# A GRU scan with a ternary FFN on one core: a bias tile loaded earlier, and ScalarE seeding the candidate's bank two steps sooner

## The reference, cut to what matters

```python
def cell(h, x):
    gi = x @ W_ih + b_ih
    gh = h @ W_hh + b_hh
    i_r, i_z, i_n = jnp.split(gi, 3, axis=-1)
    h_r, h_z, h_n = jnp.split(gh, 3, axis=-1)
    r = jax.nn.sigmoid(i_r + h_r)
    z = jax.nn.sigmoid(i_z + h_z)
    n = jnp.tanh(i_n + r * h_n)
    h_new = (1.0 - z) * n + z * h
...
wq_gu = ternary_quant(w_gate_up)      # groups of 64: mean |w| is the scale, q in {-1, 0, 1}
gate, up = jnp.split(x @ wq_gu.T, 2, axis=-1)
h = jax.nn.silu(gate) * up
out = rms_norm(h) @ ternary_quant(w_proj).T
x = x + out
```

## Time and profile before

| What | Value |
| --- | --- |
| median of 3 runs | 346.22 us (346.09 to 346.31) |
| the profiled execution | 346.3 us |
| its span, first to last instruction | 344.5 us |
| PE busy | 339.4 us (99%) |
| DVE busy | 233.6 us (68%) |
| ACT busy | 222.8 us (65%) |
| POOL busy | 184.0 us (53%) |
| granted TensorE clock, mean | 1.000 |

### The profile page before, as it was taken

One profiled execution on the slowest core, in us unless ns is written; L12 is line 12 of the kernel. 1 busy time (PEld: TensorE's weight loads), 2 busy tenths in 40 slices (PEclk: granted clock), 3 DMA queues, 4 the chain that ended last, 5 costly groups with the idle time before them and its releaser, 6 DMA issues.

```text
span 344.5 us, 5631 instructions
## 1 busy us (share of the span) xinstructions
PE 339.4 (99%) x2059; PEld 295.2 (86%) x2059; DVE 233.6 (68%) x462; ACT 222.8 (65%) x438; POOL 184.0 (53%) x156
## 2 busy tenths in 40 slices
PE   8999999999999999999999999999999999999996
PEld 4889988788988889888888889888888888888895
DVE  7578788899677565755667554875558555664866
ACT  5768888886756757555766656566564655756662
POOL 2315571465825446255454446444472554799694
PEclk9999999999999999999999999999999999999999
DMA  7994000045001000140001000010000100010101
GB/s 240 319 410 192 3 0 2 0 148 220 1 2 62 2 0 0 44 142 2 0 0 63 0 2 0 2 63 0 2 0 2 60 1 2 0 64 1 57 6 61
DMA packets 7891, 18.72 MB, mean 54 GB/s; under 512 B 564, under 2 KB 4788, under 8 KB 7352
## 3 DMA queue, kind: packets, MB, share of 16 engines
q1 hardware_dynamic: 7176, 17.97, 13.9%
q10 hardware_dynamic: 688, 0.39, 0.4%
HBM read 14.17 MB, written 4.19 MB: 53 GB/s over the span
## 4 chain that ended last, share of the span: by engine, by line
PE 94%; DVE 3%; ACT 1%; issue 1%; DVEq 0%
PE ps_ffn L1105 30%; PE ps_out L1143 16%; PE ps_rz L1017 7%; PE ps_rz L1022 7%; PE ps_rz L1018 7%; PE ps_n L1017 3%; PE ps_n L1022 3%; PE ps_n L1018 3%; PE ps_rz L1105 2%; PE ps_ffn L1270 2%; PE ps_t L1098 1%; PE ps_ffn L1017 1%; PE ps_ffn L1022 1%; PE ps_ffn L1018 1%; PE ps_n L1055 1%
## 5 line engine op out<-in xcount | busy, mean ns | idle before, releaser
L354 POOL TENSOR_TENSOR hid_lo<-work,hid_hi 128x512 fp32r<-128x512 f32 x62 | 81.7, 1317 | 103.6 <-ACT hid_hi L452 99.6
L1105 PE MATMUL ps_ffn<-st_hi,wguT 128*128 128x512 f32 x236 | 93.7, 397 | 0.3 <-DVE work L737 0.3
L1105 PE MATMUL ps_ffn<-st_lo,wguT 128*128 128x512 f32 x236 | 92.7, 393 | 0.0
L361 POOL TENSOR_TENSOR sq_sum<-sq_sum,work 128x512 f32<-128x512 f32 x55 | 73.2, 1331 | 1.8 <-ACT work L466 0.6
L737 DVE TENSOR_TENSOR work<-work,ps_ffn 128x512 f32<-128x512 f32 x55 | 37.6, 683 | 31.5 <-ACT work L448 31.5
L452 ACT CAST hid_hi<-work 128x512 fp32r<-128x512 f32 x63 | 38.8, 616 | 23.0 <-DVE work L747 23.0
L1105 PEld LDWEIGHTS ps_ffn<-st_hi,wguT 128*128 128x128 f32 x236 | 44.4, 188 | 8.3 <-DVE work L737 0.9
L1105 PEld LDWEIGHTS ps_ffn<-st_lo,wguT 128*128 128x128 f32 x236 | 44.5, 189 | 7.3
L747 DVE TENSOR_TENSOR work<-work,ps_ffn 128x512 f32<-128x512 f32 x63 | 43.2, 686 | 4.7 <-PE ps_ffn L1105 2.8
L1143 PEld LDWEIGHTS ps_out<-wpT,hid_hi 128*128 128x128 f32 x240 | 35.8, 189 | 3.7
L1143 PE MATMUL ps_out<-wpT,hid_lo 128*128 128x256 f32 x240 | 38.8, 284 | 0.0
(11 more groups left out here) (226 smaller groups left out, 716.0 us busy)
## 6 DMA issues: line engine op xcount, KB each, us to landing
out_dram<-o_st SPq DMA_DIRECT2D x7, 512.0 KB, 2.6
xT_all<-in_x_dram SPq DMA_DIRECT2D x1, 3072.0 KB, 17.6
x_ring<-in_x_dram SPq DMA_DIRECT2D x1, 3072.0 KB, 11.5
x_ring<-in_L_ffn_w_gate_up_dram SPq DMA_DIRECT2D x4, 512.0 KB, 8.9
x_ring<-in_L_ffn_w_proj_dram SPq DMA_DIRECT2D x2, 512.0 KB, 11.6
x_ring<-in_x_dram SPq DMA_DIRECT2D x1, 1024.0 KB, 5.4
work<-in_L_cond_W_ih_dram SPq DMA_DIRECT2D x3, 256.0 KB, 4.4
work<-in_L_cond_W_hh_dram SPq DMA_DIRECT2D x3, 256.0 KB, 4.6
```

What stands on the lines that cost most here:

```text
L354: nc.gpsimd.tensor_tensor(hid_lo[:, j % RING], hid[:, j % 2], f32(hid_hi[:, j % RING]), ALU.subtract).then_inc(hid_lo_ok, 1)
L361: nc.gpsimd.tensor_tensor(sq_sum[:], sq_sum[:], hid_sq[:, j % 2], ALU.add).then_inc(sq_added, 1)
L1105: mm = pe.matmul(bank, w, group_state(part, G, k), start=(k == 0 and i == 0), stop=(k == KD - 1 and i == 1))
```

## The change

Three things are done. The two DMAs of the n bias tile are issued before units 0 and 1 of the FFN weights and before the inputs of steps 4 to 7. ScalarE's `seed_n` starts at t = 0, that is for the bank of step 2, in place of step 4; TensorE's bias rows for n stay only for steps 0 and 1, and its input products for n wait for `n_seed` from step 2 on. The two halves of unit 0's signs, which stood where the two added seeds now stand, move: the first to behind `q_abs_of(0)` in step 0, the second to behind the r gate in step 2.

```diff
             load_inputs(2, 4, ld_x2)
+            for i, b in enumerate((b_ih, b_hh)):
+                sp.dma_start(bias[:, 1, i * D:(i + 1) * D], b[2 * D:G3].partition_broadcast(P)).then_inc(ld_bias_n, 16)
             load_unit(0)
             load_unit(1)
             load_inputs(4, LEAD, ld_x4)
-            for i, b in enumerate((b_ih, b_hh)):
-                sp.dma_start(bias[:, 1, i * D:(i + 1) * D], b[2 * D:G3].partition_broadcast(P)).then_inc(ld_bias_n, 16)
...
                 elif u >= 2:
                     q_weights(u - 2)
+                elif t:
+                    first_signs(1)
                 if t == 0:
                     n_gate(t)
                     z_gate(t)
                     q_abs_of(0)
+                    first_signs(0)
...
                 input_hi(t + 2)
-                if t < 2:
-                    first_signs(t)
-                elif t < LEAD - 1:
-                    if t == 2:
+                if t < LEAD - 1:
+                    if t == 0:
                         act.wait_ge(ld_bias_n, 32)
                     seed_n(t + 2)
...
             def input_n_part(t, part):
 
-                if t > 3 and part == 0:
-                    pe.wait_ge(n_seed, t - 3)
+                if t > 1 and part == 0:
+                    pe.wait_ge(n_seed, t - 1)
...
             def input_n(t):
-                if t > 3:
-                    pe.wait_ge(n_seed, t - 3)
+                pe.wait_ge(n_seed, t - 1)
...
                 input_rz(t + 1)
-                if t < 3:
+                if t < 1:
                     seed_n(t + 1)
```

## The result

Slower, by a third of one per cent: the changed kernel takes 347.49 us (median of 20 runs, 346.58 to 349.46) against 346.35 us for the kernel before (20 runs, 345.86 to 346.85). The ratio is 1.0035, 95% interval 1.0024 to 1.0046. The forecast was 347.1 with a range of 345.7 to 347.8; the measured loss is 1.14 us, forecast were 0.88.

The account below looks back on a forecast made before the run. TensorE was taken to bound the kernel. A 1.34 us wait for the late state's copy less 0.46 saved on bias rows gave +0.88: 347.2 for the profiled execution, 347.1 as median, range 345.7 to 347.8.

Parts of the forecast that it names:

- TensorE bounds and hangs on the state's copy: TensorE, busy 99%, sets the time; delay of ScalarE's transposed-state copy at step 0's end delays it by the same amount.
- No slack: Step 0's end: TensorE's first product starts some 0.1 us after the state's copy ends, so any delay passes on.
- Two pairs of bias rows: TensorE, at 19.14 and 24.70: removing the bias rows for n saves 0.23 us each, minus 0.46 together.
- ScalarE's added seeds and the second signs: ScalarE: seeds replace half signs at the ends of steps 0 and 1; second signs fit step 2's idle time; cost nothing.
- The first signs: ScalarE, step 0 before the state's copy: 0.53 us, covered by 1.10 us of idle time if nothing else changed.
- D: DMA queue: how much later unit 0 lands with the bias tile's load ahead of it, taken as 2.3 us.
- high bound: Upper limit for unit 0's delay: the tile's cost ahead of unit 2 in the earlier profile, 2.5 us.
- the prediction's cover of 0.96: ScalarE, step 0: unit 0's landing may slip 0.96 us before the state's copy is late, from there one for one.
- B: Rival: unit 0's delay is a mean DMA engine's, 1.2 to 2.1 us; time 346.0 to 346.9; chance 0.23.
- C: Rival: the slow DMA stretch is not the tile's; delay 0.7 us is hidden, 0.46 saved, time 345.8; chance 0.18.
- D (the clock falls): Rival: the stall lowers TensorE's clock from 2.4 to 1.2 GHz, adding 2.65 us, time 349.8; chance 0.05.
- rule of the Trainium skill on row pitch: Copies with rows a large power of two apart in HBM fall from 207 to 103 GB/s; tile then some 1.4 us.

Follow-up runs that it names:

- 128 rows: Changed kernel with both n bias tile DMAs reading 128 different rows of cond instead of one bias row 128 times: 345.89 against 346.38 us before.
- the two versions without a late unit 0: Changed kernel with tile loads between units 0 and 1: 345.95 us; with old load order, first signs back, step 2's seed in step 1: 345.77; before 346.38.
- signs later: Changed kernel with both halves of unit 0's signs in step 2, between r and z gates: 346.80 against 346.28 us for the kernel before.
- loads only: Kernel before with only the tile's two broadcasts moved ahead of units 0 and 1; bias rows and signs unchanged: 347.49 against 346.38 us.
- four broadcasts: Changed kernel with the tile's pair of broadcasts issued twice ahead of unit 0, one pair into an unused tile: 351.84 against 346.42 us before.
- late seed: Changed kernel with old load order, first signs at their old place, step 2's seed behind step 1's n gate: 345.77 against 346.38 us before.
- 16 rows: Changed kernel with both tile DMAs reading rows 0 to 15 of cond, each 8 times: 346.54 against 346.42 us for the kernel before.
- one row of cond: Changed kernel with both tile DMAs broadcasting row 0 of cond instead of the bias rows: 347.83 against 346.42 us for the kernel before.

## Why the prediction was right, point by point

- TensorE bounds and hangs on the state's copy: right. The copy came 2.10 us later, 0.17 of which are the later first transpose of step 0, and the wait was 1.83. "No slack" was off by 0.1 us: the product started 0.40 behind the copy's start before and 0.30 behind it here, and with 128 rows a copy 0.09 late cost nothing. So the cover is 1.06, not 0.96.
- Two pairs of bias rows, 0.46 us: right. From step 1's first transpose to step 2's are 5.29 us in the changed kernel, 5.54 before, and the two versions without a late unit 0 gain 0.4 to 0.6.
- ScalarE's added seeds and the second signs, nothing: right, shown by the same two versions.
- The first signs, free alone and paid once unit 0 is late: right, 0.5 us by the run with the signs later.
- D: the mechanism was right, the size too small. I took 2.3, with 2.5 as the high bound; the profiled execution had 3.1. By the medians the wait is 1.14 + 0.46 = 1.6 us, so D is 2.6 with the prediction's cover of 0.96, and 2.7 with 1.06. The loads only give the same: 1.1 us of loss and a cover of 0.5 more. The four profiled executions with two broadcasts ahead of unit 0 gave 2.0, 2.2, 3.1 and 3.2. My bound was a single number, the tile's cost at another place in the queue in one execution; it was no bound. With D 0.3 to 0.4 too small and the slack of 0.1 left out, the loss was forecast 0.26 us too small; that the second miss takes back a part of the first is luck.
- The rivals: B (the delay of a mean DMA engine) reached to 346.9, with 346.5 as its middle, and is under the measured 347.49; C (the slow stretch isn't the tile's) is refuted, the stretch moved with the tile and vanished with other rows as source. D (the clock falls): not in the profiled execution, where TensorE's clock stays at 1.00, but real at a longer wait, as the four broadcasts show, at 1.3 us where the prediction had put 2.65. Two of the 20 runs of the changed kernel took 349.3 and 349.5 us at a mean granted clock of 0.995, the value of the run with four broadcasts, where the others had 0.998 to 1.000. They had no trace, so this is likely and not shown.
- The rule of the Trainium skill on row pitch (DMA: Bandwidth & Descriptors, "Latency and other measured facts") is measured on copies whose rows lie far apart, and the step from there to one row was the prediction's own. It pointed the right way, but its ratio of two was too mild: the tile's estimate of 1.4 us by that ratio stands against a D of 2.6 to 2.7 by the medians.

## What to carry to other kernels

Before a load is moved ahead of others, ask what the passed loads have behind them on the engine that waits, and price the moved load by its own stretch of the trace, not by its bytes. An operation that waits also delays the work written behind it on its engine, though that has nothing to do with it: here the state's copy stood behind the quantisation. When a load must be early for one reader, moving the reader later (late seed) can give the same gain with no load moved.

## What the runs showed of the hardware

Two broadcasts from HBM, each of one 1 KB row to 128 partitions, made unit 0 behind them 2.0 to 3.2 us later in four profiled executions, where the same bytes from 128 different rows made it 0.7 later, and 16 rows each read 8 times 0.9. In the window from 9.5 to 12.5 us, in which they and their neighbours in the queue go over, all loads together moved 143 GB/s at a DMA share of 0.39 in the changed kernel, 220, 248 and 255 GB/s in the other three (one row of cond, loads only, signs later), 301 with 16 rows and 370 with 128 rows, the last two at full share.

The runs of the changed kernel lie 2.9 us apart, those of before 1.0. Without the two runs at the lower mean clock it is 1.7; that the rest comes from the spread of D is likely and not shown.

In the four broadcasts TensorE did nothing for 4.05 us in the middle of dense work. The granted clock was then 0.50 for the first 3 us of the new work, and this cost 1.3 us beyond the wait. Waits of 1.8 us (changed kernel) and 2.4 us (one row of cond) left it at 1.00.
